# A scan stage of a two-layer model on Trainium2: one quarter product in four moved from VectorE to GpSimd

## The reference, cut to what matters

```
dt = softplus(dt_r @ dt_w + dt_b)            # (b, position, channel)
def step(h, (dt_t, x_t, B_t, C_t)):
    da = exp(dt_t[..., None] * A)            # A is (channel, 16)
    h  = da * h + (dt_t * x_t)[..., None] * B_t[:, None, :]
    y  = einsum('bdn,bn->bd', h, C_t)        # sum over the 16 states
y = (scan's y + x * D) * silu(z)
```

## Time and profile before

| | us |
|---|---|
| median of the runs | 1763.95 |
| the profiled execution | 1764.51 |
| its span (first to last instruction) | 1762.7 |
| busy in the span: PE | 1363.7 |
| DVE | 1288.8 |
| ACT | 1167.2 |
| POOL | 914.5 |

### The profile page before, as it was taken

How to read it: one execution, slowest core, us unless ns; L and a number is a source line. 1 busy time by engine, 2 the same in 40 slices (tenths; PEclk the granted TensorE clock), 3 DMA queues, 4 the chain that set the end, 5 groups by cost and what they waited for, 6 DMA issues and landing times. The chain is left out here.

```text
span 1762.7 us, 16122 instructions
## 1 busy us (share of the span) xinstructions
PE 1363.7 (77%) x3950; PEld 514.5 (29%) x3950; DVE 1288.8 (73%) x1358; ACT 1167.2 (66%) x1791; POOL 914.5 (52%) x443
## 2 busy tenths in 40 slices
PE   3999938476574488884788889888888888874996
PEld 2343301011010377762222222222222222111775
DVE  1455539789798255551199999999999999993675
ACT  2566348677584256563888888888888888741554
POOL 4100016858779000000588888888888888870000
PEclk9999955555555799996878987888888888555998
DMA  5343330020200222211677677777777777633562
GB/s 142 93 124 106 87 120 17 11 86 0 97 0 31 71 74 79 77 53 54 155 174 168 165 170 162 168 171 176 174 175 175 175 174 165 152 78 80 125 165 68
DMA packets 137306, 200.03 MB, mean 113 GB/s; under 512 B 27387, under 2 KB 69629, under 8 KB 136450
## 3 DMA queue, kind: packets, MB, share of 16 engines
q1 hardware_dynamic: 135380, 196.53, 44.8%
q10 hardware_dynamic: 1854, 2.70, 0.6%
HBM read 145.55 MB, written 53.63 MB: 113 GB/s over the span
## 5 line engine op out<-in xcount | busy, mean ns | idle before, releaser
L1758 DVE TENSOR_TENSOR_SCAN m_h<-m_qa,m_state,m_ub 128x512 f32<-128x512 f32 x384 | 463.9, 1262 | 14.6 <-POOL m_ub L1370 10.9
L1370 POOL TENSOR_TENSOR m_ub<-m_dlb,m_bt 128x1536 f32<-128x1536 f32 x128 | 438.5, 3446 | 15.7 <-DVE m_h L1758 11.4
L1719 ACT ACTIVATE m_qa<-m_dlb,k_a 128x512 f32<-128x512 f32 x384 | 254.2, 682 | 89.9 <-DVE m_h L1758 88.8
L1130 POOL TENSOR_TENSOR b_u<-b_dl,b_z 128x1024 f32<-128x1024 f32 x48 | 126.0, 2628 | 246.9 <-DMA b_z<-scratch_z 200.1
L1572 PE MATMUL m_qc<-m_bcr,k_selc 32*128 32x512 f32 x256 | 166.6, 734 | 100.3 <-DVE m_g L1769 100.1
L1769 DVE TENSOR_TENSOR m_g<-m_h,m_qc 128x1536 f32<-128x1536 f32 x128 | 221.7, 1732 | 14.3 <-issue 7.7
L1589 PE MATMUL m_qy<-m_g,k_seld 128*32 128x512 f32 x768 | 176.7, 774 | 0.0
L967 PE MATMUL b_qb<-b_bc,k_pack_sel 96*128 96x512 bf16 x96 | 78.6, 819 | 108.2 <-DVE b_u L1051 108.2
L1025 ACT ACTIVATE b_qa<-b_dl,b_a 128x512 f32<-128x512 f32 x96 | 65.5, 684 | 91.5 <-DVE b_h L1066 78.6
L1349 POOL MEMSET m_cva<- 128x640 f32 x2 | 1.3, 632 | 234.4 <-POOLq L1974 234.4
L1515 PE MATMUL m_qf<-m_cva,k_conv 113*96 113x504 f32 (+1 forms) x192 | 108.2, 708 | 17.9 <-DMA m_cvb<-scratch_xpad 17.9
(11 more groups left out here) (181 smaller groups left out, 2808.5 us busy)
## 6 DMA issues: line engine op xcount, KB each, us to landing
m_dlb<-scratch_dldu SPq DMA_DIRECT2D x128, 384.0 KB, 10.2
m_bt<-scratch_brow SPq DMA_DIRECT2D x128, 256.0 KB, 5.9
scratch_dldu<-m_dldu SPq DMA_DIRECT2D x32, 384.0 KB, 3.2
scratch_z<-a_z SPq DMA_DIRECT2D x24, 256.0 KB, 5.8
b_z<-scratch_z SPq DMA_DIRECT2D x3, 2048.0 KB, 8.8
scratch_y<-b_yrow SPq DMA_DIRECT2D x12, 512.0 KB, 2.9
c_y<-scratch_y SPq DMA_DIRECT2D x16, 384.0 KB, 3.5
scratch_gate<-m_gt SPq DMA_DIRECT2D x32, 192.0 KB, 3.5
```

The costliest lines, as they stand in the source:

```text
L1130: nc.gpsimd.tensor_tensor(by_column(u[s][:], col), by_column(dl[s][:], col), seen(z[:], col, piece), ALU.mult).then_inc(u_ready, 1)
L1370: nc.gpsimd.tensor_tensor(ub[k % 3][:], dlb[u % 2][:, J:2 * J, :], bcast(bt[u % 2][:, n, :], J), ALU.mult).then_inc(ub_ready, 1)
L1719: nc.scalar.activation(q_a[:, j, :], dlb[u % 2][:, j, :], ACT.Exp, scale=G["a1"][:, j, n:n + 1]).then_inc(da, 1)
L1758: nc.vector.tensor_tensor_scan(h[k % 3][:, j, :], q_a[:, j, :], ub[k % 3][:, j, :], state[:, k % NS, j:j + 1], ALU.mult, ALU.add).then_inc ...
```

## The change

In every unit, the last of the twelve group products with C (step n = 3, third group) is done by POOL instead of DVE. POOL can't read the PSUM tile in which PE spreads C, so the four C rows of that group are loaded from memory, each repeated over 32 partitions, into a new tile ct with two buffers. For this the store of rows writes B and C rows together (32 rows instead of 16). POOL's product stands in step 0 of the next turn, behind the rounding and ahead of the ub product. PE's sums, DVE's reuse of h and SP's next load wait for a new semaphore, shared_c.

```diff
--- before.py
+++ after.py
@@ -1313,6 +1313,9 @@
         ub, h = ([m.sb(f"m_{n}{r}", [P, J, CH]) for r in range(3)] for n in ("ub", "h"))
         g = [m.sb(f"m_g{r}", [P, J, CH]) for r in range(2)]
         state = m.sb("m_state", [P, NS, J])
+        ct = [m.sb(f"m_ct{r}", [P, CH]) for r in range(2)]
+        shared_c = m.sem("m_shared_c")
+        ct_loaded = [m.sem(f"m_ct_loaded{r}") for r in range(2)]
         q_a = m.ps("m_qa", [P, J, CH])
         q_c = m.ps("m_qc", [P, CH])
         q_y, q_f, q_m = (m.ps(f"m_q{n}", [DI, CH]) for n in ("y", "f", "m"))
@@ -1396,9 +1399,19 @@
                 nc.gpsimd.tensor_tensor(dldu[v % 2][:, 1, :], dldu[v % 2][:, 0, :], xm[v % 4][0:DI, :],
                                         ALU.mult).then_inc(du_ready, 1)
 
+            def times_c(v):
+                if not exists(v):
+                    return
+                k = 4 * v + 3
+                pool.wait_ge(scanned, 3 * k + 3)
+                pool.wait_ge(ct_loaded[v % 2], 64 * (v // 2 + 1))
+                pool.wait_ge(added, k - 1)
+                nc.gpsimd.tensor_tensor(g[k % 2][:, J - 1, :], h[k % 3][:, J - 1, :], ct[v % 2][:], ALU.mult).then_inc(shared_c, 1)
+
             def step(t, s, k):
                 if s == 0:
                     rounding(t + 2)
+                    times_c(t - 1)
                 if s == 2:
                     du_of(t + 2)
                 drive(k + 2)
@@ -1437,7 +1450,7 @@
                 if not exists(v):
                     return
                 sp.wait_ge(bc_out, v + 1)
-                sp.dma_start(D["brow"][v], bcr[v % 4][DI + NS:P, :]).then_inc(brow_stored[v % 4], 16)
+                sp.dma_start(D["brow"][v], bcr[v % 4][DI:P, :]).then_inc(brow_stored[v % 4], 16)
 
             def store_drive(v):
                 if not exists(v):
@@ -1453,9 +1466,18 @@
                 if v >= 2:
                     sp.wait_ge(ub_ready, 4 * (v - 2) + 4)
                 for n in range(4):
-                    src = D["brow"][v].rearrange("(g n) t -> n g t", n=4)[n]
+                    src = D["brow"][v, NS:2 * NS, :].rearrange("(g n) t -> n g t", n=4)[n]
                     sp.dma_start(bt[r][32 * n:32 * n + 32, :, :],
                                  src.unsqueeze(0).broadcast_to([32, 4, CH])).then_inc(bt_loaded[r], 16)
+
+            def load_c(v):
+                if not exists(v):
+                    return
+                if v >= 2:
+                    sp.wait_ge(shared_c, v - 1)
+                for n in range(4):
+                    sp.dma_start(ct[v % 2][32 * n:32 * n + 32, :],
+                                 D["brow"][v, NS - 4 + n, :].unsqueeze(0).broadcast_to([32, CH])).then_inc(ct_loaded[v % 2], 16)
 
             def load_drive(v):
                 if not exists(v):
@@ -1490,6 +1512,7 @@
                 if s == 3:
                     load_rows(t + 2)
                     load_drive(t + 2)
+                    load_c(t + 2)
 
             turns(step)
             for r in range(2):
@@ -1582,6 +1605,8 @@
                     return
                 u, n = divmod(k, 4)
                 pe.wait_ge(read, k + 1)
+                if n == 3:
+                    pe.wait_ge(shared_c, u + 1)
 
                 if n == 0 and u >= 1:
                     pe.wait_ge(y_ready, u)
@@ -1753,6 +1778,8 @@
                 if k >= 3:
                     dve.wait_ge(read, k - 2)
                     dve.wait_ge(kept, k - 2)
+                    if (k - 3) % 4 == 3:
+                        dve.wait_ge(shared_c, (k - 3) // 4 + 1)
                 for j in range(J):
                     dve.wait_ge(da, 3 * k + j + 1)
                     nc.vector.tensor_tensor_scan(h[k % 3][:, j, :], q_a[:, j, :], ub[k % 3][:, j, :],
@@ -1766,7 +1793,8 @@
 
                 if k >= 2:
                     dve.wait_ge(added, k - 1)
-                nc.vector.tensor_tensor(g[k % 2][:], h[k % 3][:], bcast(q_c[:], J), ALU.mult).then_inc(read, 1)
+                own = J - 1 if k % 4 == 3 else J
+                nc.vector.tensor_tensor(g[k % 2][:, 0:own, :], h[k % 3][:, 0:own, :], bcast(q_c[:], own), ALU.mult).then_inc(read, 1)
 
             def outputs(v):
                 if not exists(v):
@@ -1952,7 +1980,7 @@
 
 SCRATCH = [("xpad", [B, C + 1, H + 2, W], F32), ("z0", [J, P, T], F32), ("dt0", [3, B * K4 * R0, T], BF16),
            ("bc0", [3, 32, T], BF16), ("dtw0", [3, B * R0 + 1, J * K4 * P], BF16), ("y0", [J, P, T], F32), ("x2", [B, C, T], F32),
-            ("gate1", [B, DI, T], F32), ("brow", [UNITS, NS, CH], F32), ("dldu", [UNITS, 2, DI, CH], F32),
+            ("gate1", [B, DI, T], F32), ("brow", [UNITS, 2 * NS, CH], F32), ("dldu", [UNITS, 2, DI, CH], F32),
             ("y1", [B, DI, T], F32)]
```

## The result

The changed kernel takes 1792.7 us (median of 4 runs, 1788.6 to 1795.2) against 1763.2 (4 runs): a ratio of 1.0165, 95% interval 1.0142 to 1.0188, so 1.7% slower. The forecast was 1788.0, with a range of 1778 to 1800. The profiled execution takes 1790.8 us, span 1789.0, 26.3 us more than the one of before.

A forecast was written before the change was run, and what follows sets the result against it. The prediction took a POOL-ACT ring of 22.21 us, not DVE, as the bound; +6.3, +17.2, +1.25 and -0.7 gave +24.0 us on 1764.51, 1788.5, less 0.56 for the median: 1788.0, range 1778 to 1800.

The forecast's parts named there:

- the ring: Second layer's scan stage: POOL and ACT wait on each other in a 22.21 us loop without slack, growing to 23.46.
- DVE is the bound: Rival, scan stage: POOL's 2.15 us wait is free time, 32 units save 0.54 us each, 1747 us; chance 0.06.
- The price of the product: POOL's new 128x512 product with C, behind the rounding, was taken to add 1.25 us per turn.
- The signs that the prediction named: Mid-stage: rounding starts 23.4 to 23.5 us apart, longer ACT and DVE waits, POOL's wait unchanged, DVE busy about 92%.
- First 13 turns: Early middle of the scan stage: 305.0 us instead of 298.7, +6.3, with PE stalls falling into DVE's idle time.
- Next 14: Later middle of the scan stage: 328.4 us instead of 311.3, +17.2.
- From unit 30's to unit 31's rounding: Turn from 1511.79 to 1535.33 us: ACT's xm waits for POOL's acc there too, +1.25 us.
- After it: End of the stage, POOL idle half the time: half of three shortened DVE products counted, -0.7 us.
- the half-hidden rival: Scan stage: ACT's xm late by less than 1.25 us, time within 0.2% of before, 1764; chance 0.04.
- old PE stalls cost nothing: First 13 turns: DVE's stalls behind PE's broadcast of C fall into its new idle 1.96 us.
- The waits of PE and the queue of SP: PE's sums waiting for POOL's product, and SP's C loads holding up the row store, were priced at nothing.
- The stalls stay: Rival: turns with PE stalls also grow 1.25 us, or late loads delay dlb; 35 us, 1799; chance 0.10.

The follow-up runs named there:

- e3: Kernel before with DVE's third-group product with C of every fourth step left out, no POOL product, no loads; 1751.6 us, ratio 0.9932.
- e1: Changed kernel with POOL's product with C placed ahead of the rounding instead of behind it; 1756.0 us, 0.9958 of the kernel before.
- e5: Kernel before with POOL's two sums of acc moved ahead of the second ub product of step 1; 1766.6 us, ratio 1.0030.
- e6: Changed kernel with POOL's two sums of acc moved ahead of the second ub product of step 1; 1744.6 us, 0.9900 of the kernel before.
- e4: Kernel before with only the change's transfers added (row store, loads of C), DVE doing all products; 1763.1 us, ratio 1.0002.
- e9: e5 with two of three matmuls of the second layer's upper convolution rows left out on PE; 1767.7 us, 1.0042 of the kernel before.
- e10: Changed kernel with two of three matmuls of the upper convolution rows left out on PE; 1799.5 us, 1.0219 of the kernel before.
- e12: e6 with PE computing the gate product three times per unit instead of once; 1752.2 us, 0.9936 of the kernel before.
- e8: Changed kernel run again unaltered, for its spread; 1791.1 us, 1.0161 of the kernel before.

## Why the prediction was right

**The ring was the bound, not DVE: shown.** e3 gives DVE the saving for nothing and the turn doesn't move; e1 takes POOL's product out of the ring and the turn goes back; e5 and e6 shorten the ring and the clean turn follows DVE. The rival "DVE is the bound" asked for turns of some 21.5 us, which only kernels with both the saving and the sums moved have.

**The price of the product: right.** 1.25 us was taken; the turn grew by 1.23, and the instruction lasts 1.27. DVE's product got 0.53 us shorter (0.54 taken).

**The signs that the prediction named: seen.** DVE's wait for q_a is 1.80 us in clean turns ("near 2"), ACT's for acc 62.5 us in 26 waits, 2.4 each ("over 2"), POOL's for lw 2.15 ("unchanged"), DVE's busy share 92% ("about 92%"). DVE's own work was put 0.08 us too high: 22.04 and 21.50 us a turn, where e5 and e6 show 21.96 and 21.42.

**The sum, term by term.** First 13 turns: forecast 305.0, measured 305.1 (904.16 to 1209.23). Next 14: forecast 328.4, measured 329.1, with the three turns of 24.0 us in both stretches together. From unit 30's to unit 31's rounding: +1.25 forecast, +0.42 measured. After it: -0.7 forecast and -0.7 measured (227.4 to 226.7). The prediction read the turn from unit 30 to 31 wrongly: it held not only xm's wait for acc, but also 1.59 us in which ACT waits for PE further on in the ring (L1693, at 1529.48). In the changed kernel this wait is 0.79 us (at 1556.44), so 0.80 of the 1.25 vanished in it, which is the half-hidden rival in one turn. Sum inside the stage 24.0 against some 24.0. That it fits to a tenth is luck: this term came out 0.8 us below the forecast and the 27 turns ahead of it 0.8 us above (the three turns of 24.0 us, which the sum didn't have, add 1.7, and a ring of 23.43 instead of 23.46 takes 0.8 of that back). What the profile has above this, 2.3 us at unit 3's rounding, doesn't come from the change: the stage had started 2.9 us later already (819.08 and 816.18 us). That is the difference ahead of the stage that goes with the clock there (0.50 and 0.51 from 400 to 600 us). Both profiles of the changed kernel start late, so the traces don't show that each execution draws it anew. The medians are 29.5 us apart and not 26.3 or 24.0; the interval (25 to 33 us) leaves out the forecast by a microsecond. I can't settle that rest with profiles of single executions.

**That old PE stalls cost nothing: right, but not altogether.** They fall into DVE's new idle time, except where PE, behind at the low clock, holds up ACT inside the ring, 0.6 us a time.

**The waits of PE and the queue of SP: right.** DVE's waits for PE ahead of its output are 4.8 us in four places from 900 to 1570 us; PE never waits for POOL. SP waits 192.7 us in 29 places for POOL's product before it issues the loads of C, as priced, and still nothing waits for dlb or bt.

**GpSimd beside VectorE.** The scans take 1262 ns and the ub products 3442 with the new product beside them, 1262 and 3447 without. That agrees with the rule of the Trainium skill (GPSIMD Engine Reference, section 1), by which DVE instructions in a two-port mode or with two SBUF inputs contend with GpSimd. Each of VectorE's instructions in this stage reads a PSUM tile, so no run here shows what happens with two SBUF inputs.

**The loads: free, shown by e4.** "The stalls stay" (1799) didn't happen.

**What the prediction lacked.** It knew the ring and DVE as the two limits and took PE for covered. e5 shows a third one close by: without the ring, the kernel before isn't faster. e6's gain rests on DVE's shorter work, and it too has turns stalled by PE.

## What to carry to other kernels

An engine at 99% can still be paced by others: where the same small wait comes back every turn, follow it round through the engines and add up the lengths; if they make the period, only what lies on that path counts. Idle time that is part of such a ring can be filled only by work put ahead of the wait, where the inputs are there; here the same instruction one place later cost its full length. After such a move look for the next limit before the gain is booked.

## What the hardware did that I had not expected

Less work for TensorE brought a lower granted clock, and more work a higher one: 0.86 to 0.79 (e5 to e9), 0.83 to 0.76 (changed to e10), 0.86 to 0.91 (e6 to e12), over the same 595 us. It is not one lucky profile: over the whole kernel e5's executions have 0.783 to 0.790 and e9's 0.749 to 0.763, the changed kernel's 0.772 to 0.777 and e10's 0.747 to 0.755, e6's 0.786 to 0.791 and e12's 0.799 to 0.812. A mean of 0.79 is a mixture of the two levels, 1.2 and 2.4 GHz: in the kernel before, a pair of matmuls of the broadcast takes 2.07 us at 1149.29 (granted clock 0.50 there) and 1.12 us at 1156.95 (1.00).

The spread of one kernel's times goes with the clock as well: of the 17 executions of the kernel before that stand beside e5 to e8, the one with the lowest clock (0.777) is the slowest (1771.1 us) and the one with the highest (0.797) the fastest (1750.3). Which is cause and which effect, these runs don't separate.

The relation isn't a strict one (e1 has 0.90 with 1395 matmuls in that stretch, e6 0.86 with 1402), and what sets it stays open. e9 and e10 also compute other values than the kernel does, which e12 doesn't. But in this stage nobody can count on winning time by taking matmuls away.
